# A graph network kernel: live groups spread over the attention sums, kept rows across stage boundaries, one wait for every lookup

## What is computed

```python
def _gat_conv(h, src, dst, W, a_src, a_dst, bias):
    g = h @ W
    s = (g * a_src).sum(-1)
    d = (g * a_dst).sum(-1)
    e = jax.nn.leaky_relu(s[src] + d[dst], NEG_SLOPE)
    m = jax.ops.segment_max(e, dst, num_segments=N)
    ...
    alpha = ex / z[dst]
    out = jax.ops.segment_sum(g[src] * alpha[:, None], dst, num_segments=N)
    return out + bias
...
    src_emb = x[src]
    weight_input = jnp.concatenate([src_emb, rel_emb, time_mask], axis=-1)
    h = jax.nn.relu(weight_input @ W1 + b1)
    dynamic_weights = jax.nn.sigmoid(h @ W2 + b2)
    message = src_emb * rel_emb * dynamic_weights
    q = (x[dst] @ Wq + bq).reshape(-1, NUM_HEADS, HEAD_DIM)
    k = (message @ Wk + bk).reshape(-1, NUM_HEADS, HEAD_DIM)
    v = (message @ Wv + bv).reshape(-1, NUM_HEADS, HEAD_DIM)
    scores = (q * k).sum(-1) / HEAD_DIM ** 0.5
```

## Time and profile before

| | us |
|---|---|
| median of 3 runs | 7478.26 |
| lowest, highest | 7476.2, 7483.27 |
| the profiled execution | 7526.6 |
| its span, first to last instruction | 7524.8 |

### The profile page before, as it was taken

The page is one execution under the profiler, slowest core; times in us unless marked ns, Lnnn a source line. Parts: engine busy times, 40 slices in busy tenths (PEclk is TensorE's granted clock), DMA queues, the critical chain, the costliest instruction groups (busy, mean ns, idle before and its releaser), DMA issues. The chain is left out here.

```text
span 7524.8 us, 103556 instructions
## 1 busy us (share of the span) xinstructions
PE 3807.2 (51%) x29228; PEld 3250.7 (43%) x29332; DVE 3611.2 (48%) x11040; ACT 1525.8 (20%) x3908; POOL 4016.6 (53%) x4360
## 2 busy tenths in 40 slices
PE   2544365544445232334455577777777574333346
PEld 1433255433345232334444465566666462233334
DVE  3366555576644123333344555555555992222225
ACT  0244300244300002000000333333333122000003
POOL 6355565355555654666665444444443245666662
PEclk8655578755567556565556788888888896555658
DMA  5355466455455443555552344444444451111111
GB/s 150 97 164 161 135 199 192 132 166 169 144 158 177 123 134 80 134 142 151 156 160 76 119 139 137 137 139 139 137 140 129 125 171 49 45 45 45 45 45 34
DMA packets 564725, 944.22 MB, mean 125 GB/s; under 512 B 122022, under 2 KB 226111, under 8 KB 563599
## 3 DMA queue, kind: packets, MB, share of 16 engines
q1 hardware_dynamic: 263779, 403.40, 16.9%
q0 software_dynamic: 140576, 316.92, 16.6%
q10 hardware_dynamic: 159840, 217.27, 10.1%
HBM read 703.64 MB, written 235.53 MB: 125 GB/s over the span
## 5 line engine op out<-in xcount | busy, mean ns | idle before, releaser
L259 POOL DMA_INDIRECT s_rows<-rel_tab,src_v x832 | 786.3, 945 | 811.3 <-DVE s_msg L2495 538.2
L259 POOL DMA_INDIRECT stash<-gat_tab,src_g x784 | 763.8, 974 | 570.5 <-issue 365.7
L259 POOL DMA_INDIRECT stash<-in_x,src_g x736 | 721.3, 980 | 493.1 <-issue 230.8
L259 POOL DMA_INDIRECT gcn_rows<-gcn_tab,src_g x784 | 756.3, 965 | 427.3 <-issue 235.8
L259 POOL DMA_INDIRECT ggn_rows<-ggn_tab,src_g x784 | 743.6, 948 | 424.1 <-issue 227.3
L1619 PE MATMUL e_psb<-tmp,e_oh 128*128 x3328 | 621.0, 351 | 684.9 <-DVE e_oh L1587 414.8
L1619 PEld LDWEIGHTS e_psb<-tmp,e_oh 128*128 128x128 f32 x3328 | 548.8, 250 | 757.4 <-issue 756.2
L1172 PE MATMUL g_psc<-g_parts,g_oh 128*128 128x52 bf16 x9408 | 509.9, 221 | 632.5 <-DVE g_oh L1091 323.6
L1952 PE MATMUL ggn_pso<-ggn_rows,ggn_oh 128*128 x1952 | 395.5, 379 | 695.0 <-DVE ggn_oh L1869 312.0
L1172 PEld LDWEIGHTS g_psc<-g_parts,g_oh 128*128 128x128 bf16 x9408 | 435.7, 120 | 707.2 <-DVE g_oh L1091 358.8
L1952 PEld LDWEIGHTS ggn_pso<-ggn_rows,ggn_oh 128*128 128x128 f32 x1952 | 359.3, 279 | 731.8 <-issue 729.6
(11 more groups left out here) (506 smaller groups left out, 8714.9 us busy)
## 6 DMA issues: line engine op xcount, KB each, us to landing
edge_v<-stash SPq DMA_DIRECT2D x392, 256.0 KB
g_lo_rows<-lo_rows ACTq DMA_DIRECT2D x392, 256.0 KB
e_values<-edge_v SPq DMA_DIRECT2D x392, 256.0 KB
oh_dram<-tmp ACTq DMA_DIRECT2D x208, 256.0 KB
s_oh<-oh_dram SPq DMA_DIRECT2D x208, 256.0 KB
edge_v<-acc SPq DMA_DIRECT2D x208, 256.0 KB
r_values<-edge_v SPq DMA_DIRECT2D x208, 256.0 KB, 3.0
tmp<-drel_rows ACTq DMA_DIRECT2D x208, 128.0 KB
```

The costliest lines, as they stand in the source:

```text
L259: pool.indirect_dma_start(rows[:, t, :], None, tab[:, :], bass.IndirectOffsetOnAxis(ap=edges[:, t:t + 1], axis=0)).then_inc(s_land, 16)
```

## The change

Six things change together.

1. *Live groups are spread.* `LIVE[l]` names them: from group 4 on, evenly, up to 12 groups before the end. `KEPT_ORDER[l]` has the others. Layer 0 keeps 121 groups and has 75 live ones, layer 1 keeps 84 and has 112. The early lookups take the groups of `KEPT_ORDER`.
2. *Live rows stay in SBUF.* VectorE reads a live group from `stash` as soon as its lookups have landed; it is neither stored nor loaded. Its slot is free when VectorE has used it (`s_wv`).
3. *No stop at the boundaries.* The slots' semaphores (`kept_landed`, `kept_stored`) belong to the layer and not to the stage. SP ends a stage without waiting for stores, and leaves the stores of the last three kept groups (`LATE = 3`) to the next stage. The blocks of the preparation, the logits and the softmax have `no_gpsimd_drain=True`.
4. *Every lookup waits by itself.* In the logits and in `gat_sums` the count of TensorE's work that a lookup waits for is worked out for each lookup, not for each group. In `gat_sums` it is also 40 tiles earlier than before.
5. *The scores.* The first lookup of iteration n+4 waits for the messages of n as before, the second for their transposes, the third for the queries, the fourth for the values.
6. *Numbers.* `EARLY` 7 and not 5, `KEPT_FIRST` 13 and not 12, and the shares of the stages as in `KEPT`.

```diff
-EARLY = 5
-KEPT_FIRST = 12
-KEPT_PREP = 36
-KEPT = ((KEPT_PREP, 115, 126), (0, 76, 86))
+EARLY = 7
+KEPT_FIRST = 13
+KEPT_PREP = 37
+KEPT = ((KEPT_PREP, 112, 121), (0, 75, 84))
+LEAD_IN, LEAD_OUT = 4, 12
+LATE = 3
+LIVE = tuple([LEAD_IN + j * (GROUPS - LEAD_IN - LEAD_OUT) // (GROUPS - k[2]) for j in range(GROUPS - k[2])] for k in KEPT)
+KEPT_ORDER = tuple([g for g in range(GROUPS) if g not in live] for live in LIVE)
...
-        def gather_group(pool, rows, tab, edges, s_land):
+        kept_landed = [[top.enter_context(nc.semaphore(f"layer{l}_landed{k}")) for k in range(KEEP)] for l in range(2)]
+        kept_stored = [[top.enter_context(nc.semaphore(f"layer{l}_kept{k}")) for k in range(KEEP)] for l in range(2)]
+
+        def gather_group(pool, rows, tab, edges, s_land, s_pace=None, pace=None):
 
             for t in range(GT):
+                if s_pace is not None and pace(t) > 0:
+                    pool.wait_ge(s_pace, pace(t))
                 pool.indirect_dma_start(rows[:, t, :], None, tab[:, :], bass.IndirectOffsetOnAxis(ap=edges[:, t:t + 1], axis=0)).then_inc(s_land, 16)
...
-        def keep_rows(sp, first, n, s_land, s_st):
-
-            for j in range(n):
-                keep_store(sp, first + j, j // KEEP, j % KEEP, s_land, s_st)
-            for k in range(min(n, KEEP)):
-                sp.wait_ge(s_st[k], ((n - 1 - k) // KEEP + 1) * 16)
+        def keep_rows(sp, l, first, last):
+
+            for j in range(first, last):
+                keep_store(sp, l, j)
...
                 def lookups(j):
 
-                    return RING + (j - 2) * GROUPS // (last - first) if j > 2 else 0
-
-                with nc.Block() as block:
+                    return RING + (j - 2 * GT) * GROUPS // ((last - first) * GT) if j > 2 * GT else 0
+
+                with nc.Block(no_gpsimd_drain=True) as block:
...
-            def added(j):
-
-                return GT * (j * (ITERS - 28) // live)
+            live, kept = LIVE[l], KEPT_ORDER[l]
+
+            def added(i):
+
+                return max(0, i * (ITERS - 28) // len(live) - 40)
...
-                        keep_gathers(pool, gat_src(l), first, live, k_land, k_st, s_o, added)
+                        for j, g in enumerate(live):
+                            k = (len(kept) + j) % KEEP
+                            if j >= KEEP:
+                                pool.wait_ge(s_wv, live[j - KEEP] + 1)
+                            else:
+                                pool.wait_ge(kept_stored[l][k], (len(kept) + j) // KEEP * 16)
+                            pool.sem_inc(s_turn, 1)
+                            gather_group(pool, stash[:, k, :, :], gat_src(l), src_g[:, g * GT:(g + 1) * GT], kept_landed[l][k],
+                                         s_o, lambda t: added(j * GT + t))
...
+                        for c, g in enumerate(kept):
+                            if c == LOADED:
+                                keep_rows(sp, l, len(kept) - LATE, len(kept))
+                            if c >= LOADED:
+                                sp.wait_ge(s_wv, kept[c - LOADED] + 1)
+                            sp.wait_ge(kept_stored[l][c % KEEP], c // KEEP * 16 + 16)
+                            sp.dma_start(vr[:, c % LOADED, :, :], edge_v[g * P:(g + 1) * P, :].rearrange("p (t d) -> p t d", d=D)).then_inc(s_val[c % LOADED], 16)
...
                             if n < GROUPS:
-                                dve.wait_ge(s_val[k % LOADED], i * (WSLOTS // LOADED * 16) + (k // LOADED + 1) * 16)
+                                if n in live:
+                                    j = live.index(n)
+                                    m = len(kept) + j
+                                    dve.wait_ge(kept_landed[l][m % KEEP], (m // KEEP + 1) * (16 * GT))
+                                    values = stash[:, m % KEEP, :, :]
+                                else:
+                                    c = kept.index(n)
+                                    dve.wait_ge(s_val[c % LOADED], c // LOADED * 16 + 16)
+                                    values = vr[:, c % LOADED, :, :]
...
-                            gather_group(pool, rows[:, n % RING, :, :], rel_tab, src_v[:, n * GT:(n + 1) * GT], s_row[n % RING])
+                            for t in range(GT):
+                                if n >= RING and t >= 1:
+                                    pool.wait_ge((s_mt, s_q, s_v)[t - 1], n + 1 - RING)
+                                pool.indirect_dma_start(rows[:, n % RING, t, :], None, rel_tab[:, :],
+                                                        bass.IndirectOffsetOnAxis(ap=src_v[:, n * GT + t:n * GT + t + 1], axis=0)).then_inc(s_row[n % RING], 16)
```

86 lines of the change are left out of this document (30 added, 56 removed).

## The result

The changed kernel takes 6939.13 us (median of 4, 6935.04 to 6940.38) against 7477.23 for the kernel before (4 runs, 7472.63 to 7483.27): ratio 0.9285, 95% interval 0.9268 to 0.9302, faster by 7.2%. The forecast was 7000 us, 6.4% less, range 6640 to 7330. The profiled execution spans 6933.2 us and stands, unlike that of before, at its median.

A forecast was written before the change was run, and what follows sets the result against it. No engine bounded it: GpSimd's row lookups slowed TensorE in five stages, and the vector engine waited for TensorE. Terms of -57, -119, -80, -60 and -162 took 7526.6 to 7049; less 48, rounded: 7000 us, range 6640 to 7330.

The forecast's parts named there:

- The scores: Scores stage: spreading a group's four lookups takes a quarter of the stall, iteration 6.8 us instead of 7.57; -162 us.
- The logits: Logits of both layers: runs of 1 or 2 lookups, 0.4 us lost a lookup, 2.45 us a group; -80 and -60.
- Stop and sums of layer 0: Softmax end and attention sums of layer 0, costed together by GpSimd's sequence: end at 1377 instead of 1434, -57 us.
- of layer 1: Softmax end and attention sums of layer 1, costed together: end at 2732 instead of 2852, -119 us.
- the price of a live group: Attention sums: 5.4 us a live group, between GpSimd's floor of 5.0 and the 6.1 of the kernel before.
- The tail: Attention sums after the last live group: 26 visits at 1.87 us, with the finish 52 us.
- The rest: Seven early groups, `KEPT_FIRST` 13, no wait for last stores in the first two stages, fewer transfers: 0 us.
- From execution to median: Whole kernel: 48 us taken off 7049, as the profiled execution stood 48 us above the median of 7478.
- The third rival: Chance 0.05: live groups cost 5.0 us plus undisturbed steps, logits and scores unchanged, 7683 us; decides from 6.34 a group.
- The stop's own gain: Start of each attention sums stage: vector engine's wait before its first memset under 5 us instead of 31.93 and 26.60.
- the first, short runs nearly free: Rival, chance 0.18: short lookup runs cost TensorE almost nothing, scores 5.3 us an iteration; -957, 6520 us.
- The second, only the number of lookups counts: Rival, chance 0.27: lookups' number and pauses, not run length, set TensorE's loss; scores unchanged; -192, 7286 us.

The follow-up runs named there:

- scores_late: Changed kernel, but all four lookups of a group in the scores released together by the transposes of iteration n-4: 6944.2 us, ratio 0.9298.
- logits_alone: Kernel before, with only the logits' lookups held one by one, on the other kind of chip: 5913.22 us, ratio 0.9997.
- rows_by_sp: Kernel before, with the scores' rows brought by SP's plain loads of consecutive rows, GpSimd idle in that stage: 6803.77 us, ratio 0.9111.
- stop_back: Changed kernel with the stop after both softmaxes back, on the other kind of chip: 5898.97 us, ratio 0.9975.
- sums_free: Changed kernel without the lookups' waits on TensorE's tile count in the attention sums: 7024.92 us, ratio 0.9408.
- scores_alone: Kernel before, with only the scores' new waits for transposes, queries and values, on the other kind of chip: 5912.56 us, ratio 0.9996.

## Why the prediction was right

By its own steps, on the profiled executions (7526.6 to 6935.0 us, -591.6 measured, -478 forecast):

- *The scores*, forecast -162, measured -329. The direction was right, the term was mis-sized, and its picture was wrong. I let "spreading take a quarter" of a stall of 0.83 us a lookup. Nothing was spread: the lookups stayed in runs of four, but each now begins at the transposes, and the loss is 1.82 us a run instead of 3.32 and, in the 55 runs of eight, 7.09. The stall is 6.07 - 4.24 = 1.83, 0.46 a lookup. scores_late shows that one release point does it all. That the change helped by another way than the one it was made for was luck. At 6.07 GpSimd works 5.0 of it, so little is left.
- *The logits*, forecast -80 and -60, measured -103 and -81. Right in mechanism; 0.4 us a lookup was (479.5 - 20 - 196 x 1.83) / 300 = 0.34. Short runs are cheaper than runs of four, as the nine single lookups had hinted. That the pacing brought it is argued, not shown: logits_alone was to show it and fell on the other kind of chip. The 16 and 4 lookups less are worth at most 14 and 4 us of it, at 0.9 each.
- *Stop and sums of layer 0*, forecast -57, measured -3 (softmax -27, sums +24), and *of layer 1*, forecast -119 (its own figures give -120), measured -62 (-21 and -40). Here the step that failed is the price of a live group: 5.4 us, "nearer the floor because no rows go through memory for them any more". Counted from 45 us after the softmax's start, where the forecast had GpSimd through with its 36 kept lookups, it took 443 and 650 us to the last one (1261.3 and 2541.3 us): 5.9 and 5.8 us a group. The tail behind took 69 and 67 instead of 52. That is 75 x 0.5 + 17 = 54 and 112 x 0.4 + 15 = 60 us, the misses of 54 and 57.
- *The rest*, forecast 0, measured -14. It is the net of two stages of lookups that the change doesn't touch (-12.5 and -8.6) and of a few us more elsewhere. The first is no gain: rows_by_sp, which has the code of before there, takes 1194.6 us like the changed kernel (1194.7), where the profiled execution of before takes 1207.2. It also has 556 and 759 us for the logits and sums of layer 1, where that execution has 561 and 764. So the measured gains of the stages above hold a few us each of that one long execution.
- *From execution to median* I took off 48 us, since that of before stood so far above its median; the one of after stands 4 below its own. So the sum was 113 us too small, the correction 52 too large, and the forecast of 7000 ended 61 us above 6939. The scores' miss of 167 us and the sums' of 54 and 57 pulled against each other too. So the total came nearer than its terms, and that was luck.

Why a live group stayed at 5.9: the prediction has VectorE waiting for rows because they go through memory, and takes the price near the floor since they no longer do. That reading of the row was wrong. It names a store, `edge_v<-stash`, for which VectorE has no wait in the code; the semaphore behind it had that use in an earlier stage. By the updates in the trace, 448 of the 471 us that VectorE sat idle before this line in the sums of layer 1 ended with TensorE's tile count (286 of 290 behind 2450 us). With the detour gone it waits as before (waits of VectorE in the sums of layer 1, changed kernel):

```profile
DVE tmp L1586 <- DMA p_early_edges<-in_src: 304.0, 43, 18.2
DVE tmp L1586 <- PE e_psb L1621: 79.0, 36, 5.2
```

309.5 us became 304.0, and the name is again that of an earlier use: of 433 us of such waits 414 end with the tile count and 15 with a landing in a stash slot. The detour had not been holding the stage; TensorE's late counts were, and are. On the other kind of chip it is the reverse (stop_back, same stage: 57 of 320 us end with the count, 262 with landings). The third rival was argued down with the same misread row.

GpSimd meanwhile is idle, between 1937 and 2450 us, for 180.9 us before 353 lookups. At 0.30 us each between back-to-back ones that leaves 75 us of real pauses, 0.85 a group, on 5.0. In the pause VectorE catches up, with the counts that have then come in.

Put in the terms of the table: a run of n lookups takes 1.25 n us and lets some 4.5 us of work through; the visits that belong to it need n x 1.61 / 4 x 1.27; the rest of them is done in the pause. For n = 12.5 in layer 1: 15.6 + 6.4 - 4.6 = 17.4 us (measured 16.4 for 12 and 17.8 for 13), 5.6 a group. The mean of 5.8 includes single lookups within the pauses. For n = 20 in sums_free: 25 + 10.2 - 4.9 = 30.3, 6.1; measured 30.37 on average. For the scores, n = 4: 5.0 + 4.24 - 3.2 = 6.04, measured 6.06. The longer the run, the larger the share of the visits left for the pause. (The amount let through is itself from these runs, so this is a check of the accounting and no proof.) In the sums the amount is near what VectorE's lead of four visits holds, 4 x 1.27 = 5.1 us, so a longer lead might let more through. No run tested that, and in the scores, where the lead is four iterations, only 3.2 us get done.

The stop's own gain was right where it stood, 5.01 us of wait instead of 31.93, and much of it was given back where that was forecast, behind GpSimd's backlog (the share was measured on the other kind of chip alone): in the 44.6 us after the start TensorE did 48 matmuls, under 33 lookups (windows, all engines):

```profile
811.50:856.10 44.60, 15.32 (x48) 10.90 (x48) 9.55 (x23) 0.89 (x4) 30.21 (x33) 0.54 0.44 126
```

The rivals: the first, short runs nearly free, needed runs of one and two everywhere, which the change made in the logits alone, and at 0.33 us a lookup they are cheap there, not free. The second, only the number of lookups counts, is refuted for the sums by sums_free (same lookups, 82 us more in the two stages) and for the scores by scores_late (same lookups and bytes as before, 325 us less). The third, slower, needed 6.34 us a live group. sums_free got near, with 6.06.

The Trainium skill, "Runtime: NRT & Kernel Launch", section "Instruction fetch mechanics", has instructions refilled in blocks mostly behind the work. The page of each kernel, part 3, lists that traffic, here of the kernel before on the chip of the prediction:

```profile
q8 instruction: 279, 4.57, 0.3%
q14 instruction: 251, 2.06, 0.1%
```

scores_alone and logits_alone, which are the kernel before but for one edit each, have these two rows unchanged on the chip without the stall: the same packets, the same shares. So the stall is not more refilling; whether a refill's effect on TensorE is slower there, no row tells. Late counts explain the waits in the sums without it. The pauses that show only "issue" (128.2 us in one line of the scores above) they don't explain by themselves, and those stay open.

## What to carry to other kernels

Where GpSimd's lookups slow TensorE, treat a run of them as a window in which a fixed few microseconds of work get done: keep runs to four or fewer, and try where in TensorE's work each one begins, since one well-placed wait took 325 us here. When an engine waits for a count, look up whose count it is in the code before believing the name that a view gives to the wait: here a name of an earlier use hid that VectorE waited for TensorE. A pacing wait on a count that advances in bursts releases in bursts; and a buffer read in place has to be spread over the work, since it takes away the producer's freedom to run ahead. Before tuning against such a stall, run the kernel on more than one chip: 7% on one was within 0.5% on the other, as far as the nearest versions measured there show (0.9949 to 0.998; the changed kernel itself was not run on it).

For the kernel itself, the changed one with the tight lead has the lowest time on the kind of chip of the prediction (6922.85 us, though the intervals of the two ratios overlap), and with sixteen more kept groups in layer 1 it is the fastest version on the other (5884.91 us). The second was not run on the first chip.

## What the hardware showed that I had not expected

- The same program takes 5915 us on some chips and 7470 on others, in every run there (25 runs from 5910.98 to 5919.78 us on one, 7 from 7462.64 to 7486.09 on another), 21% apart. A lookup takes GpSimd the same on both (0.946 and 0.945 us in the scores), the two stages compared that have no lookups (the softmax and the sums of the relations) agree to 0.2 us, and all of the difference lies in stages with lookups. What differs between the chips is not settled: nothing in the profile names it. Three chips showed the fast kind, one of them twice, and none showed both.
- On the kind with the stall, a run of four lookups cost 1.82 us in the changed kernel's scores, a run of twenty 20.1 in sums_free.
- There TensorE's semaphore updates come in late while lookups run, one in about 2 us in the sums of sums_free, and 0.04 us apart once the lookups pause. Nothing of the kind shows in rows_by_sp on the same kind of chip, or in any stage compared on the other.
- The granted clock follows the stall: TensorE in the scores had 0.83 of full speed before, 0.99 after, 0.93 in scores_late with nearly the same time. So 0.06 of clock was worth at most 4 us there; what 0.83 cost before was not measured by itself.
